# LSTM of images 1 to 3: one sigmoid for input and forget gate, one product for both, and the input products of two steps together

## What is computed

```python
x_gates = jnp.einsum('ntc,gc->ntg', y, W_ih) + b_ih + b_hh
def step(carry, xg):
    h, c = carry
    g = xg + h @ W_hh.T
    i, f, gg, o = jnp.split(g, 4, axis=-1)
    c = jax.nn.sigmoid(f) * c + jax.nn.sigmoid(i) * jnp.tanh(gg)
    h = jax.nn.sigmoid(o) * jnp.tanh(c)
    return ((h, c), h)
```

## Time and profile before

| | us |
|---|---|
| three timed runs | 5221.74, 5246.77, 5258.37 (median 5246.77) |
| the profiled execution | 5189.45, its span 5187.6 |
| TensorE, VectorE, ScalarE, GpSimd busy | 2740.8, 2181.9, 1129.5, 2570.3 |
| from first to last hidden product, images 0, 1, 2, 3 | 253, 509, 522, 523 |
| mean granted TensorE clock | 0.62 |

### The profile page before, as it was taken

One profiled execution on the slowest core, in us unless ns is written; L12 is line 12 of the kernel. 1 busy time (PEld: TensorE's weight loads), 2 busy tenths in 40 slices (PEclk: granted clock), 3 DMA queues, 4 the chain that ended last, 5 costly groups with the idle time before them and its releaser, 6 DMA issues.

```text
span 5187.6 us, 53724 instructions
## 1 busy us (share of the span) xinstructions
PE 2740.8 (53%) x19674; PEld 2081.7 (40%) x19674; DVE 2181.9 (42%) x4593; ACT 1129.5 (22%) x3009; POOL 2570.3 (50%) x2614
## 2 busy tenths in 40 slices
PE   6889556646665566646555546665655631100102
PEld 4678334435554334435544334444544421100101
DVE  6644445434333555534333454544333442321322
ACT  4544222212222122222222122222222110000000
POOL 1000445445555445545554645544554667677574
PEclk9899766655555656655555656655555655555555
DMA  7410434312111344312111243412111211111111
GB/s 223 119 35 1 125 108 120 98 47 58 36 36 48 110 122 119 100 46 61 36 39 36 88 127 110 129 52 66 36 37 33 93 56 53 51 52 50 37 52 41
DMA packets 192847, 374.01 MB, mean 72 GB/s; under 512 B 59312, under 2 KB 89264, under 8 KB 192576
## 3 DMA queue, kind: packets, MB, share of 16 engines
q1 hardware_dynamic: 108632, 200.11, 12.7%
q0 software_dynamic: 82944, 170.04, 12.4%
q10 hardware_dynamic: 1008, 0.43, 0.0%
HBM read 265.15 MB, written 104.33 MB: 71 GB/s over the span
## 4 chain that ended last, share of the span: by engine, by line
another core or an unknown queue 27%; DVE 18%; PE 17%; issue 14%; POOL 7%; ACT 4%; DMA 0%; SPq 0%; DVEq 0%; POOLq 0%; ACTq 0%
POOL got L582 7%; PE gates L1441 4%; DVE got L857 4%; DVE red L859 2%; PE bank L1358 2%; PE bank L1251 2%; DVE mx L941 2%; PE gates L1327 1%; PE bank L1302 1%; DVE samp L862 1%; PE gates L1341 1%; ACT tcell L733 1%; PE bank L1292 1%; PE bank L1497 1%
## 5 line engine op out<-in xcount | busy, mean ns | idle before, releaser
L582 POOL DMA_INDIRECT got<-sample_table,index x2592 | 2556.9, 986 | 2554.2 <-DVE red L859 1245.1
L1441 PE MATMUL gates<-hist,whh 128*128 128x96 f32 x3040 | 642.4, 379 | 163.5 <-DVE hist L1111 132.4
L1251 PE MATMUL bank<-turned,wout 128*128 128x96 f32 x1728 | 348.5, 385 | 687.8 <-issue 277.8
L1441 PEld LDWEIGHTS gates<-hist,whh 128*128 128x128 f32 x3040 | 571.0, 281 | 262.2 <-DVE hist L1111 202.5
L1251 PEld LDWEIGHTS bank<-turned,wout 128*128 128x128 f32 x1728 | 334.8, 297 | 704.9 <-DVE turned L866 371.8
L1421 PE MATMUL gates<-xs,wa 128*128 128x192 bf16 (+1 forms) x776 | 252.7, 326 | 492.2 <-ACT sig L731 229.9
L857 DVE TENSOR_TENSOR got<-got,weight 128x1152 f32<-128x1152 f32 x288 | 388.0, 1347 | 260.9 <-DMA got<-sample_table,index 252.4
L941 DVE TENSOR_REDUCE mx<-gates 128x2 f32<-128x392 f32 x576 | 298.9, 556 | 463.6 <-remote 257.0
L1358 PE MATMUL bank<-pt,v 98*18 98x128 f32 x4608 | 287.3, 351 | 186.9 <-issue 143.0
L1103 DVE TENSOR_TENSOR prod<-sig,gc 128x96 f32<-128x96 f32 x384 | 96.3, 251 | 608.4 <-ACT sig L725 359.9
L658 ACT ACTIVATE pt<-gates 98x512 f32<-98x512 f32 x384 | 219.8, 595 | 471.7 <-remote 244.8
(11 more groups left out here) (137 smaller groups left out, 3671.2 us busy)
## 6 DMA issues: line engine op xcount, KB each, us to landing
kst<-k_parts SPq DMA_DIRECT2D x96, 441.0 KB
got<-sample_table,index POOLq DMA_INDIRECT x2592
qst<-q_parts SPq DMA_DIRECT2D x96, 288.0 KB
k_parts<-kp SPq DMA_DIRECT2D x24, 882.0 KB
k_parts<-kp SPq DMA_DIRECT2D x24, 588.0 KB
q_parts<-qp SPq DMA_DIRECT2D x24, 576.0 KB
sample_table<-tab SPq DMA_DIRECT2D x8, 1568.0 KB
q_parts<-qp SPq DMA_DIRECT2D x24, 384.0 KB
```

The costliest lines, as they stand in the source:

```text
L582: pool.indirect_dma_start(out=got[:, uu % RING, n, :], out_offset=None, in_=tables[p], in_offset=bass.IndirectOffsetOnAxis(ap=at, axis=0)) ...
L1251: mm = pe.matmul(out_ps[n % 2][:, at:at + GN], wout[:, tap, :], turned[:, k % 2, tap, :], start=(tap == 0), stop=(tap == NTAP - 1))
L1441: pe.matmul(gate[n][:, h:h + W], whh[:, HID * GATE_OF[n]:HID * (GATE_OF[n] + 1)], hist[:, (t - 1) % HIST, :], start=False, stop=True, skip ...
```

## The change

For images 1 to 3 (`p > 0`) the gates stand in the order candidate, input, forget, output (`BOTH_GATE_OF`), so that input and forget gate lie in neighbouring banks, and all gates use the same half. ScalarE takes one sigmoid of both (128 x 2 x 96) when the forget gate is there, and VectorE one product of `sig[:, 0:2]` with `gc` (candidate and cell state side by side), 192 columns. TensorE makes the input products of two steps for all four gates at once after odd steps, behind the output sigmoid (`both_inputs`, twelve matmuls), and none after even steps. Image 0 keeps its code.

```diff
--- before.py
+++ after.py
@@ -45,6 +45,7 @@
 CHUNK = max(b - a for a, b in CHUNKS)
 LIN = 8
 GATE_OF = (1, 2, 0, 3)
+BOTH_GATE_OF = (2, 0, 1, 3)
 WARM = 10
 HIST = 16
 
@@ -357,6 +358,8 @@
         g_done = sem("g_done")
         i_done = sem("i_done")
         o_done = sem("o_done")
+        if_done = sem("if_done")
+        if_act = sem("if_act")
         f_act = sem("f_act")
         g_act = sem("g_act")
         i_act = sem("i_act")
@@ -721,14 +724,23 @@
                 for t in range(W):
                     tt = W * p + t
                     h, late = W * (t % 2), W * ((t + 1) % 2)
-                    act.wait_ge(f_done, tt + 1)
-                    act.activation(sig[:, 0, :], gate[0][:, h:h + W], ACT.Sigmoid).then_inc(f_act, 1)
-                    act.wait_ge(g_done, tt + 1)
-                    act.activation(gc[:, 0, :], gate[1][:, h:h + W], ACT.Tanh).then_inc(g_act, 1)
-                    act.wait_ge(i_done, tt + 1)
-                    act.activation(sig[:, 1, :], gate[2][:, late:late + W], ACT.Sigmoid).then_inc(i_act, 1)
-                    act.wait_ge(o_done, tt + 1)
-                    act.activation(sig[:, 2, :], gate[3][:, late:late + W], ACT.Sigmoid).then_inc(o_act, 1)
+                    if p == 0:
+                        act.wait_ge(f_done, tt + 1)
+                        act.activation(sig[:, 0, :], gate[0][:, h:h + W], ACT.Sigmoid).then_inc(f_act, 1)
+                        act.wait_ge(g_done, tt + 1)
+                        act.activation(gc[:, 0, :], gate[1][:, h:h + W], ACT.Tanh).then_inc(g_act, 1)
+                        act.wait_ge(i_done, tt + 1)
+                        act.activation(sig[:, 1, :], gate[2][:, late:late + W], ACT.Sigmoid).then_inc(i_act, 1)
+                        act.wait_ge(o_done, tt + 1)
+                        act.activation(sig[:, 2, :], gate[3][:, late:late + W], ACT.Sigmoid).then_inc(o_act, 1)
+                    else:
+                        act.wait_ge(g_done, tt + 1)
+                        act.activation(gc[:, 0, :], gate[0][:, h:h + W], ACT.Tanh)
+                        act.wait_ge(if_done, tt - W + 1)
+                        act.activation(sig[:, 0:2, :], gates_all[:, 512:1536].rearrange("p (g m) -> p g m", g=2)[:, :, h:h + W],
+                                       ACT.Sigmoid).then_inc(if_act, 1)
+                        act.wait_ge(o_done, tt + 1)
+                        act.activation(sig[:, 2, :], gate[3][:, h:h + W], ACT.Sigmoid).then_inc(o_act, 1)
                     act.wait_ge(cell_done, tt + 1)
                     act.activation(tcell[:, :], gc[:, 1, :], ACT.Tanh).then_inc(tanh_done, 1)
                     for k, at in ((2, 2), (3, 10)):
@@ -1099,12 +1111,18 @@
                     dve.wait_ge(later_in, 16 * 4)
                 for t in range(W):
                     tt = W * p + t
-                    dve.wait_ge(f_act, tt + 1)
-                    dve.tensor_tensor(prod[:, 1, :], sig[:, 0, :], gc[:, 1, :], ALU.mult).then_inc(prods_done, 1)
-                    dve.wait_ge(g_act, tt + 1)
-                    dve.wait_ge(i_act, tt + 1)
-                    dve.tensor_tensor(prod[:, 0, :], sig[:, 1, :], gc[:, 0, :], ALU.mult).then_inc(prods_done, 1)
-                    dve.wait_ge(prods_done, 2 * (tt + 1))
+                    if p == 0:
+                        dve.wait_ge(f_act, tt + 1)
+                        dve.tensor_tensor(prod[:, 1, :], sig[:, 0, :], gc[:, 1, :], ALU.mult).then_inc(prods_done, 1)
+                        dve.wait_ge(g_act, tt + 1)
+                        dve.wait_ge(i_act, tt + 1)
+                        dve.tensor_tensor(prod[:, 0, :], sig[:, 1, :], gc[:, 0, :], ALU.mult).then_inc(prods_done, 1)
+                        dve.wait_ge(prods_done, 2 * (tt + 1))
+                    else:
+                        dve.wait_ge(if_act, tt - W + 1)
+                        dve.tensor_tensor(prod[:, :, :].rearrange("p k n -> p (k n)"), sig[:, 0:2].rearrange("p k n -> p (k n)"),
+                                          gc[:, :, :].rearrange("p k n -> p (k n)"), ALU.mult).then_inc(prods_done, 1)
+                        dve.wait_ge(prods_done, W + tt + 1)
                     dve.tensor_tensor(gc[:, 1, :], prod[:, 0, :], prod[:, 1, :], ALU.add).then_inc(cell_done, 1)
                     dve.wait_ge(o_act, tt + 1)
                     dve.wait_ge(tanh_done, tt + 1)
@@ -1409,6 +1427,29 @@
 
             def lstm(p):
 
+                def both_inputs(first):
+                    for k, (begin, _) in enumerate(CHUNKS):
+                        if first == begin:
+                            pe.wait_ge(xs_in[k], 64 * (p + 1))
+                    wait(pe, o_act, W * p + first)
+                    xin = xs[:, :, first:first + 2, :].rearrange("p j t f -> p t j f")
+                    for n, g in enumerate(BOTH_GATE_OF):
+                        w = slice(HID * g, HID * (g + 1))
+                        pe.matmul(gate[n], wa[:, w], xin, start=True, stop=False, skip_group_check=True)
+                        pe.matmul(gate[n], wb[:, w], xin, start=False, stop=False, skip_group_check=True)
+                        mm = pe.matmul(gate[n], bw[0:96, w], ones[0:96, :], start=False, stop=(first == 0), skip_group_check=True)
+                        if first == 0 and n != 1:
+                            mm.then_inc((g_done, None, if_done, o_done)[n], 1)
+
+                def both_recurrence(t):
+                    pe.wait_ge(hid_done, W * p + t)
+                    h = W * (t % 2)
+                    for n, g in enumerate(BOTH_GATE_OF):
+                        mm = pe.matmul(gate[n][:, h:h + W], whh[:, HID * g:HID * (g + 1)], hist[:, (t - 1) % HIST, :], start=False, stop=True,
+                                       skip_group_check=True)
+                        if n != 1:
+                            mm.then_inc((g_done, None, if_done, o_done)[n], 1)
+
                 def inputs(first, last, gates):
                     for k, (begin, _) in enumerate(CHUNKS):
                         if first <= begin < last:
@@ -1459,12 +1500,21 @@
                     pe.wait_ge(later_in, 16 * 4)
                 pe.wait_ge(bias_ones, p + 1)
                 pe.wait_ge(steps_in, 32 * (p + 1))
-                inputs(0, 2, (0, 1))
-                inputs(0, 1, (2, 3))
+                if p == 0:
+                    inputs(0, 2, (0, 1))
+                    inputs(0, 1, (2, 3))
+                else:
+                    both_inputs(0)
                 for t in range(W):
-                    if t > 0:
-                        recurrence(t)
-                    inputs_ahead(t)
+                    if p == 0:
+                        if t > 0:
+                            recurrence(t)
+                        inputs_ahead(t)
+                    else:
+                        if t > 0:
+                            both_recurrence(t)
+                        if t % 2 == 1 and t + 1 < W:
+                            both_inputs(t + 1)
                     if t % LIN == 0 and t > 0:
                         linear(t // LIN - 1)
                     elif p == 0:
```

## The result

The changed kernel takes 5157.40 us (median of six runs, 5135.21 to 5165.93) against 5242.03 us of the kernel before (six runs, 5216.19 to 5258.37): ratio 0.9841 [0.9821, 0.9861], 1.6% faster. The forecast of 5284 us had the wrong sign, and the time lies outside the range.

The account below looks back on a forecast made before the run. It took a chain of waits in the LSTM of images 1 to 3, no engine full, as the bound. Terms 5 - 1 + 11.5 - 3 = +12.5 us an image, +37 for three, gave 5284 us; range 5190 to 5345.

Parts of the forecast that it names:

- Parts 1 to 3: Merged sigmoid and product, LSTM of images 1 to 3: quiet step 0.11 us longer, +5 us an image; unit steps -1.
- rival 4: LSTM steps: the removed sigmoid's and product's fixed parts were on the chain; 94 us less, 5153 us; chance 0.05.
- Part 4: Twelve input matmuls after odd steps delay the next recurrence 0.9 us where uncovered: 13 times, +11.5 us an image.
- Part 5: Output linear layer, every eighth step, directly follows an even recurrence, done before the hidden product: -3 us an image.
- the convolutions: Sampling convolutions after odd and even steps: the bunch lengthens one and shortens the other equally, so nothing.
- rival 3: Twelve inputs directly between two recurrences lift TensorE's clock in quiet steps: 5284 - 117 = 5167 us; chance 0.08.
- Part 6: Late stretches in the LSTM: TensorE's instruction count is unchanged and stretches end with the gathers, so no change.
- Rival 2: Three TensorE signals a step instead of four shrink late stretches by a quarter: 79 us in all, 5205 us; chance 0.10.
- Rival 1: Late stretches catch the bunch of twelve in the LSTM: 94 us more for three images, 5378 us; chance 0.22.

Follow-up runs that it names:

- together only: Kernel before with input products of two steps made together, but four separate gate activations and two products: 0.9907 (5194.78 us) in late condition; 0.9987, 0.9995, 1.0003 in quiet.
- the thinned kernel after: Changed kernel with one gather instead of nine for each unit the LSTM stages order: 4762.14 us, 0.9193 of the kernel before, late condition.
- merge only: Changed kernel with input products split again, six matmuls behind each step: against the kernel before 0.9907 (5191.74 us) in late condition; 1.0029, 1.0037, 1.0041 in quiet.

## Why the prediction was wrong

**Parts 1 to 3, the merge on the chain: right in kind, small in size.** The quiet step grew by 0.11 us where it was looked at, and in the quiet condition no gain came from the removed instructions (rival 4). Over all quiet steps it is more: 230 + 173 us become 245 + 183 in 126 intervals, 0.20 us each, and with -7 us on the units the whole is +20 instead of +12. The granted clock, 0.58 to 0.59 against 0.62 to 0.64 in the traces, went down with it; that the rest comes from there was not tried.

**Part 4, the bunch: right, with its two factors off against each other.** In the step looked at the next recurrence starts 0.88 us after its hidden product would have let it (1225.39 against 1224.20 + 0.31), and the step is 0.77 us longer. Over the first traces of the quiet condition the exposed bunches, 34 plain ones and 15 behind convolutions, cost 23.7 + 15.6 = 39.3 us, where the sum had 34.5: 49 bunches at 0.80 us instead of 39 at 0.9 (it had left out those in late steps, and here there are none). Covered ones cost nothing, as it said.

**Part 5 and the convolutions: a gain put at nothing.** The output layer gained 12 us for three images (predicted 9). "The bunch makes the one longer and the other shorter by as much, so nothing" failed: convolutions behind even steps, which now have no inputs between them and the recurrence, gained 33.5 us, and those behind odd steps lost 15.6, which part 4 already holds. So a gain of 33.5 us had been put at nothing. The plain even steps and the covered odd ones gained 3.5 + 2.0 us; the granted clock stood at 0.65 to 0.68 meanwhile. That is rival 3 in a small form. Its counter-argument, that TensorE is busy without a gap either way and has less work in relation to time, was no ground for the clock to stay. Together the bunch is 23.7 + 15.6 - 33.5 - 11.7 - 3.5 - 2.0 = -11.4 us in the first trace and -7 in the mean, where +25 had been forecast.

**Part 6, "late stretches: I take nothing", is the step that turned the sign.** With the chain as it is, +3 instead of +37, the time would still have been 5245. What remains, some 85 us in the timed runs, comes only where signals are late: the same change is worth 1.0004, 1.0016 and 1.0003 where they are not. The reason given, that stretches end with the gathers, was half right. They need the gathers (thinned, all are gone), but their length also goes by what the engines do in them (twenty small matmuls more a step: 396 to 488 us in late steps; the change itself: 396 to 331). The term was also read too small: 105 us of image 1 stood for each image, and the same waits are 131 and 160 us in images 2 and 3. Rival 2 came nearest, with 79 us and a chance of 0.10, but that its number is so near is luck: together only, with all four signals, gains 46 us as well. It was set aside because four signals came at once in the earlier trace rows, which shows how one stretch ended and nothing on how long it had been. I read one late step and took from it a rule for all. That the lateness isn't the profile's doing was right: the thinned kernel after stands at 0.9193 of before in timed runs, the full one at 0.9841.

**Rival 1** (the bunch caught by late stretches, +94 us) is refused by together only: -46 us timed, and the trace agrees. By steps set beside their quiet ones, the intervals that hold the bunch carry 242 us of late excess against 218 in the kernel before, and the others 178 against 205: what one half loses the other gains, which was its counter-argument.

**What stays open.** Whether the merge shortens late stretches by its missing signals or by its missing instructions and waits: the run with more signals met the quiet condition. How much of the 46 us of the bunch is clock and how much fewer late steps: both were seen (0.58 to 0.61 against 0.55 or 0.56, and 69 late steps against 77), but its trace has only 11 us in the LSTM. How far late stretches vary from execution to execution, since no kernel has a second trace in the late condition. And what the condition is.

## What to carry to other kernels

Where a trace shows waits that end "remote", far longer than the work ahead of them, don't cost them at nothing because the change leaves the number of instructions alone: they made up 424 of 1553 us here, and a change that moved the chain by 3 us moved the time by 85. Read them in every stage that has them and over every wait of a step: one image or one wait misleads. Cost the chain and the late waits apart, and measure each half of a change by itself. Put work that nobody waits for where the engine would idle anyhow, but look at the steps that already hold something else: taking six matmuls out from between a convolution or an output layer and the next recurrence gave 33 + 12 us, and the bunch of twelve cost 24 where nothing covered it and 16 behind convolutions.

## What the runs showed of the hardware

- The same program takes 5240 us or 4040 us, by a condition of the machine that comes and goes. In the slower one ScalarE's first wait for TensorE in a late step was 5.3 to 7.9 us where it was looked at (the earlier trace rows; after: 5.34 and 7.93) instead of 1.19, in steps near runs of gathers; one gather a unit instead of nine ends it in that stage (no late wait left in 285 steps), and twenty small matmuls a step that nobody waits for lengthen it (396 to 488 us in late steps). Why is not known.
- In the quicker condition GpSimd's gathers are 49% of the chain that ended last, and the LSTM's differences reach the total in part: +20 us in the LSTM of merge only are +12 to +16 us in time, -7 us of together only are -6 to 0. A bound that lateness hides can lie right under the one that is seen.
- TensorE's mean granted clock in the LSTM rises with the same matmuls in one bunch of twelve instead of two of six: 0.62 to 0.68 in image 3 in the quiet condition, 0.55 to 0.61 in the late one. With the merge alone it falls to 0.58 in the quiet one and stays at 0.55 or 0.56 in the late one.
- A sigmoid of 192 PSUM columns from two banks takes 330 ns against 250 for 96, as 0.83 ns a column of the earlier trace rows gave; a product of 192 columns takes 350 against 256, 0.98 ns a column against the 1.04 taken.
